# Graph attention layer: two more steps gather x alone, and VectorE and TensorE take the work of a step in another order

## What is computed

```python
hl = x @ Wl.T + bl
hr = x @ Wr.T + br
s = (jnp.take(hl, src, axis=0) + jnp.take(hr, dst, axis=0)) * alpha
s = jnp.where(s >= 0, s, SLOPE * s)
smax = jax.ops.segment_max(s, dst, num_segments=n_nodes)
e = jnp.exp(s - jnp.take(smax, dst, axis=0))
denom = jax.ops.segment_sum(e, dst, num_segments=n_nodes)
att = e / jnp.take(denom, dst, axis=0)
msg = jnp.take(x, src, axis=0) * att
# out = layernorm(x + segment_sum(msg, dst))
```

## Time and profile before

| | us |
|---|---|
| median of 3 runs | 1437.57 |
| lowest and highest run | 1435.41, 1439.32 |
| span of the profiled execution | 1129.4 |
| what lies around the span (median less span) | 308.2 |
| PE busy, weight loads busy | 1079.0, 1014.7 |
| DVE busy | 1072.6 |
| ACT busy | 998.6 |
| POOL busy | 820.7 |

### The profile page before, as it was taken

How to read it: one execution, slowest core, us unless ns; L and a number is a source line. 1 busy time by engine, 2 the same in 40 slices (tenths; PEclk the granted TensorE clock), 3 DMA queues, 4 the chain that set the end, 5 groups by cost and what they waited for, 6 DMA issues and landing times.

```text
span 1129.4 us, 34988 instructions
## 1 busy us (share of the span) xinstructions
PE 1079.0 (96%) x9403; PEld 1014.7 (90%) x9403; DVE 1072.6 (95%) x1526; ACT 998.6 (88%) x2606; POOL 820.7 (73%) x858
## 2 busy tenths in 40 slices
PE   6879999999999999999999999999999999999984
PEld 5779999999999999999999999999999899999863
DVE  7889999999999999999999999999999999999967
ACT  4359999999999999999999999999999889998996
POOL 5577777777777777777777777777777777777770
PEclk9889999999999999999999999999999999999997
DMA  9887776666667776767766666677676666676533
GB/s 227 290 221 191 192 187 191 190 188 188 191 187 191 189 189 187 192 189 190 189 189 188 189 191 190 188 189 188 191 189 185 186 188 182 187 191 183 143 99 114
DMA packets 231064, 211.97 MB, mean 188 GB/s; under 512 B 46375, under 2 KB 204286, under 8 KB 230788
## 3 DMA queue, kind: packets, MB, share of 16 engines
q0 software_dynamic: 39872, 108.39, 35.5%
q1 hardware_dynamic: 190442, 100.03, 32.4%
q10 hardware_dynamic: 565, 1.33, 0.4%
HBM read 198.95 MB, written 11.47 MB: 186 GB/s over the span
## 4 chain that ended last, share of the span: by engine, by line
PE 51%; POOL 26%; issue 11%; ACT 3%; DVE 2%; DMA 0%; ACTq 0%; POOLq 0%; DVEq 0%
POOL xg L435 25%; PE ps_w L654 19%; PE ps_sT L590 11%; PE ps_u L630 9%; PE ps_z L608 5%; PE ps_q L599 2%; PE ps_u L636 2%; PE ps_qT L618 2%; ACT attr L853 1%; DVE stats L1161 1%; ACT acc L802 0%; DMA xg<-gather_rows,srcT 0%; ACT right L811 0%; DVE acc L1086 0%; ACT ex L749 0%
## 5 line engine op out<-in xcount | busy, mean ns | idle before, releaser
L435 POOL DMA_INDIRECT xg<-gather_rows,srcT x808 | 764.9, 947 | 253.0 <-issue 235.9
L654 PE MATMUL ps_w<-onehot,ex 128*128 128x128 f32 x3328 | 405.7, 275 | 1.2 <-ACT acc L806 1.2
L654 PEld LDWEIGHTS ps_w<-onehot,ex 128*128 128x128 f32 x3328 | 388.4, 192 | 1.8 <-issue 1.6
L1095 DVE TENSOR_TENSOR_SCAN ps_F<-line,B,ps_sT 128x512 f32<-128x512 bf16 x208 | 266.1, 1279 | 1.0 <-issue 1.0
L1100 DVE TENSOR_TENSOR_SCAN B<-line,ps_F 128x512 f32<-128x512 bf16 x208 | 254.0, 1221 | 7.2
L630 PEld LDWEIGHTS ps_u<-right,onehotT 128*128 128x128 f32 x1664 | 208.5, 192 | 18.9 <-issue 0.2
L630 PE MATMUL ps_u<-right,onehotT 128*128 x1664 | 221.1, 276 | 0.0
L802 ACT ACTIVATE acc<-ps_w 128x768 f32 x208 | 168.7, 811 | 23.5
L1105 DVE TENSOR_TENSOR z<-ps_sT,B 128x512 f32<-128x512 f32 x208 | 143.9, 692 | 7.1
L1121 DVE TENSOR_TENSOR ex<-ps_z,xg 128x512 f32<-128x512 f32 x208 | 141.7, 681 | 5.7 <-ACT ps_z L773 5.7
L1129 DVE TENSOR_TENSOR v<-ps_u,attr 128x512 f32<-128x512 f32 x208 | 141.8, 682 | 0.3
(11 more groups left out here) (264 smaller groups left out, 1164.1 us busy)
## 6 DMA issues: line engine op xcount, KB each, us to landing
attr<-edge_attr_in SPq DMA_DIRECT2D x832, 64.0 KB
line<-step_lines SPq DMA_DIRECT2D x182, 128.0 KB
xg<-gather_rows,srcT POOLq DMA_INDIRECT x808
gather_rows<-acc SPq DMA_DIRECT2D x12, 512.0 KB, 6.0
line<-soon_lines SPq DMA_DIRECT2D x26, 128.0 KB
edge<-step_lines SPq DMA_DIRECT2D x182, 4.0 KB
acc<-x_in SPq DMA_DIRECT2D x6, 448.0 KB, 7.6
xg<-x_in SPq DMA_DIRECT2D x6, 448.0 KB, 5.6
```

Of the source, the lines that this page charges most:

```text
L435: pool.indirect_dma_start(out=xg[:, k % SLOTS, i, :], out_offset=None, in_=rows_dram, in_offset=bass.IndirectOffsetOnAxis(ap=srcT[:, k * W ...
L654: last = nc.tensor.matmul(columns, ex[:, (k - 1) % 2, c, i, :], onehot[:, (k - 1) % 3, i, :], start=(i == 0), stop=(i == WIDE - 1), skip_g ...
L1095: V.tensor_tensor_scan(ps_F[:, :], line[:, k % LINES, 0:GE], ps_sT[:, :], B[:, (k - 1) % 3, GE - 1:GE], ALU.add, ALU.max).then_inc(F_ok, 1)
```

## The change

- `AHEAD` is 8 instead of 6: steps 6 and 7 gather x alone too. They need two more transposes, copies and products by Wl; POOL's loop over whole rows begins with step 8. PE's `ahead` waits for the copy before the last one from k = 5 on (`ahead_sb`, k - 1). `ahead(5)`, `ahead(6)` and `ahead(7)` stand one behind another after `body(0)`, on PE and on ACT.
- The negated borders of `lines` are made by ScalarE instead of VectorE, one `body` later than ScalarE's two other parts stood; VectorE's `body(-2)` and `body(-1)` stand inside its preparation of the lines; the square lies in `ex` instead of `v`.
- VectorE's `body(k)`: F, B, h, z, v, message.
- TensorE's `body(k)`: sT, qT, u, z, q, sums.
- POOL waits for `v_ok` of step k - lead + 1 instead of `z_ps` of step k - lead.

The number of instructions on PE and ACT stays as it is but for the kinds; the diff's core:

```diff
-    AHEAD = 6
+    AHEAD = 8
...
-        sq = v[0:PR, :, :, :].rearrange("p a i d -> p a (i d)")
+        sq = flat(ex[:, 1, :, :, :])[0:PR, :].rearrange("p (a d) -> p a d", a=2)
...
+                if k == 7:
+                    pool.wait_ge(srcf_ok, 2)
+                    pool.wait_ge(step_ok, 1)
                 for i in range(WIDE):
                     pool.indirect_dma_start(
                         out=xg[:, k, i, 0:D], out_offset=None, in_=x,
...
             for k in range(AHEAD, STEPS):
-                if k == 7:
-                    pool.wait_ge(srcf_ok, 2)
-                    pool.wait_ge(rel_ok, 1)
+                if k == AHEAD:
                     pool.wait_ge(ahead_ps, 3)
-                if k == 8:
                     pool.wait_ge(u_ps, 2)
...
                 if k >= lead:
-                    pool.wait_ge(z_ps, k - lead + 1)
+                    pool.wait_ge(v_ok, k - lead + 2)
...
-                if k == 5:
-                    pe.wait_ge(ahead_sb, 4)
+                if k >= 5:
+                    pe.wait_ge(ahead_sb, k - 1)
...
-                if has(k):
-                    j = k % EDGES
...
-                    last.then_inc(q_ps, 1)
-                    pe.wait_ge(z_ok, k + 1)
...
-                    last.then_inc(z_ps, 1)
                 if has(k + 4):
                     j = (k + 4) % EDGES
...
                     last.then_inc(u_ps, 1)
+                if has(k):
+                    pe.wait_ge(z_ok, k + 1)
...
+                    last.then_inc(z_ps, 1)
+                    j = k % EDGES
...
+                    last.then_inc(q_ps, 1)
                 if k == STEPS - 1:
                     opening(0)
...
                 if k == 0:
-                    ahead(5)
+                    for a in range(5, AHEAD):
+                        ahead(a)
...
-                if k == -4:
+                if k == -3:
                     act.wait_ge(rel_ok, 1)
+                    nc.scalar.activation(lines[:, :, 0, :], halves(diff), ACT.Copy, scale=-BIG).then_inc(high_ok, 1)
+                    act.wait_ge(rel_ok, 2)
...
-            V.tensor_scalar(diff[:, :, 0], row(12), -1.0, 1.0, ALU.mult, ALU.add)
+            V.tensor_scalar(diff[:, :, 0], row(12), -1.0, 1.0, ALU.mult, ALU.add).then_inc(rel_ok, 1)
+            body(-2)
...
             V.tensor_tensor(sq, halves(rel2), halves(rel2), ALU.mult).then_inc(sq_ok, 1)
-            V.tensor_scalar(lines[:, :, 0, :], halves(diff), -BIG, None, ALU.mult).then_inc(lines_ok, 1)
+            body(-1)
```

More of the change, by code:

```diff
@@ L638, in body @@
                     last.then_inc(u_ps, 1)
+                if has(k):
+                    pe.wait_ge(z_ok, k + 1)
+                    if k == 0:
+                        pe.wait_ge(src_sb, 2)
+                    if k >= 1:
+                        pe.wait_ge(msg_ok, k)
+                    for i in range(WIDE):
+                        last = nc.tensor.transpose(ps_z[:, i * D:(i + 1) * D], z[:, k % 2, i * P:(i + 1) * P], ident[:, :])
+                    last.then_inc(z_ps, 1)
+                    j = k % EDGES
+                    if k >= 1:
+                        pe.wait_ge(oh_ok, k)
+                    for i in range(WIDE):
+                        last = nc.tensor.matmul(ps_q[:, i * P:(i + 1) * P], edge[:, j, i * P:(i + 1) * P], node[:, :],
+                                                start=(i == 0), stop=(i == WIDE - 1), skip_group_check=True)
+                    last.then_inc(q_ps, 1)
                 if k == STEPS - 1:
@@ L823, in _ @@
                     nc.scalar.activation(lines[:, :, 2, :], sq, ACT.Copy).then_inc(high_ok, 1)
-                if k == -3:
-                    act.wait_ge(lines_ok, 4)
+                if k == -2:
+                    act.wait_ge(lines_ok, 3)
+                    act.wait_ge(high_ok, 3)
                     act.dma_start(line_dram[SOON:STEPS].rearrange("(p s) c -> p (s c)", s=2),
@@ new lines, in body @@
+            def body(k):
+                if has(k):
+                    dve.wait_ge(line_in[k % LINES], 16 * (k // LINES + 1))
+                    dve.wait_ge(sT_ps, k + 1)
+                    if k >= 1:
+                        dve.wait_ge(B_ok, k)
+                    V.tensor_tensor_scan(ps_F[:, :], line[:, k % LINES, 0:GE], ps_sT[:, :],
+                                         B[:, (k - 1) % 3, GE - 1:GE], ALU.add, ALU.max).then_inc(F_ok, 1)
+                    dve.wait_ge(F_ok, k + 1)
+                    if k >= 2:
+                        dve.wait_ge(gap_ok, k - 1)
+                    V.tensor_tensor_scan(B[:, k % 3, ::-1], line[:, k % LINES, GE:0:-1], ps_F[:, ::-1], -BIG,
+                                         ALU.add, ALU.max).then_inc(B_ok, 1)
+                if has(k + 2):
+                    j = (k + 2) % SLOTS
+                    dve.wait_ge(rows_in[j], 16 * (WIDE - 1) * ((k + 2) // SLOTS + 1))
+                    dve.wait_ge(u_ps, k + 3)
+                    if k + 2 < AHEAD:
+                        V.tensor_tensor(u_of(ps_u), u_of(ps_u), both[:, :, :].broadcast_to([P, WIDE, D]), ALU.add).then_inc(h_ok, 1)
+                    else:
+                        V.tensor_tensor(u_of(ps_u)[:, 1:WIDE, :], u_of(ps_u)[:, 1:WIDE, :], xg[:, j, 1:WIDE, D:ROW], ALU.add)\
+                            .then_inc(h_ok, 1)
+                if has(k):
+                    dve.wait_ge(B_ok, k + 1)
+                    if k >= 2:
+                        dve.wait_ge(z_ps, k - 1)
+                    V.tensor_tensor(z[:, k % 2, :], ps_sT[:, :], B[:, k % 3, :], ALU.subtract).then_inc(z_ok, 1)
+                if has(k + 2):
+                    j = (k + 2) % ATTRS
+                    dve.wait_ge(attr_in[j], 64 * ((k + 2) // ATTRS + 1))
+                    dve.wait_ge(h_ok, k + 3)
+                    if k >= 0:
+                        dve.wait_ge(sT_ps, k + 1)
+                    V.tensor_tensor(v[:, k % 2, :, :], u_of(ps_u), attr[:, j, :, :], ALU.mult).then_inc(v_ok, 1)
+                if k == STEPS:
+                    ratio(0)
+                if has(k - 1):
+                    dve.wait_ge(e2_ok, k)
+                    if k >= 3:
+                        dve.wait_ge(sums_ps, k - 2)
+                    V.tensor_tensor(ex[:, (k - 1) % 2, 1, :, :], u_of(ps_z),
+                                    xg[:, (k - 1) % SLOTS, :, 0:D], ALU.mult).then_inc(msg_ok, 1)
+                if k == STEPS:
+                    for c in range(1, EARLY):
+                        ratio(c)
@@ L1067, in _ @@
             sources(0)
-            dve.wait_ge(high_ok, 2)
+            dve.wait_ge(high_ok, 3)
             V.tensor_tensor(lines[:, :, 3, :], sq, lines[:, :, 2, :], ALU.subtract).then_inc(lines_ok, 1)
@@ L1134, in _ @@
-            u_of = lambda bank: bank[:, :].rearrange("p (i d) -> p i d", i=WIDE)
-            for k in range(-2, STEPS + 1):
+            for k in range(STEPS + 1):
                 body(k)
```

81 lines of the change are left out of this document (14 added, 67 removed).

## The result

The changed kernel takes 1781.75 us (median of 4 runs, 1770.91 to 1784.11), the kernel before beside it 1438.44 us (4 runs, 1435.41 to 1439.35). The ratio is 1.239, with a 95% interval of 1.2345 to 1.2435. The forecast was 1443.6 us and a range up to 1452: wrong by far.

What follows compares the result with a forecast made beforehand. VectorE was taken to bound two thirds of the loop, GpSimd the rest. Span 1129.4 - 0.3 (start) + 5.6 (loop) + 0.7 (last part) = 1135.4; with 308.2 around it 1443.6 us, range 1434.5 to 1452.

Steps and rivals of the forecast that it cites:

- with the 308.2 that lie around the profiled span: Last step of the sum: 308.2 us outside the profiled span, added to the forecast span of 1135.4 to give 1443.6.
- `v_ok` instead of `z_ps` lets GpSimd go a step earlier and is never last while slots bind: GpSimd's gate in the loop: gathers may go a step earlier, but gather slots decide; no time was given to it.
- changes nothing in the closed loop: TensorE's new order in the loop: sT stays in front, so z, sT, F keep 2.00 us; only `ps_z` comes later.
- The loop closes through TensorE at 4.91 a step: Steps 6 to 203: F waits 0.19 us for sT each step; 4.91 us a step, +5.6 us in all.
- its four parts: VectorE's step in the loop: z to F 2.00, F to B 1.31, B to h 1.14, h to z 0.46 us.
- The waits for rows: In the loop, VectorE's h waiting for GpSimd's gathered rows: 8.7 us, forecast to go.
- A: Rival, loop: F doesn't wait for sT and GpSimd's gathers end it; about 1436 us, not slower; chance 0.15.
- B: Rival, loop: slot wait not met, GpSimd keeps most of its 7.8 us head start; 1429.8 to 1433 us; chance 0.05.
- C: Rival, VectorE's loop: h doesn't start early behind scan B; B to h 1.26, step 5.03, 1467 us; chance 0.10.
- The start, -0.3: Up to F of step 6: at 96.0 against 96.25, so -0.3 us, bounds -3 and +2.
- The last part, +0.7: Behind step 203: ScalarE is never idle and its exp comes later; +0.7 us, between 0 and 1.

## Why the prediction was wrong, point by point

**The step that failed first** is "with the 308.2 that lie around the profiled span". A span of 1129.4 and a median of 1437.57 don't belong to the same kind of execution. The prediction took the difference for a constant and added it. In the runs of the changed kernel 1.8 to 3.0 us lie around it. The two spans of the kernel before, 1129.4 and 1409.9, are 280.5 us apart: 261.5 of it between F of step 6 and F of step 203 (1.33 us in each of 197 steps, 6.21 less 4.88), 17.8 ahead of that and 1.2 behind it. This is time inside the program, in waits that the first trace hardly contains. Every term was priced in a condition in which TensorE's signals come at once. The times to be forecast came from the other.

**The term that carries the miss** follows from it, and the sum had it at nothing: "`v_ok` instead of `z_ps` lets GpSimd go a step earlier and is never last while slots bind". On a chip without late signals it is worth nothing indeed (ratio 0.9994, 0.9996 and 1.0003 on three chips). On one with them it costs 26% by itself: GpSimd waits 687.2 us for v in 133 places. The prediction put no bound on this edit, for lack of a row in which the gate was last. No rival had it. TensorE's order, of which it says that it "changes nothing in the closed loop", costs 5% there by itself, and 1.45% on a chip without late signals (a step of 4.96 in place of 4.88).

**Right, where the trace's condition held.** On the chip without late signals the changed kernel took 0.20% longer (0.09 to 0.31); the sum said 6.0 us on 1129.4, or 0.5%. From span to span, 1129.4 and 1137.0, it is 7.6 us, but the kernel before is itself slower beside the second: 1134.07 us, where a span of 1129.4 stands for some 1131.2 (1.8 around it). Some 3 us of the 7.6, and of the terms below, may be that. The terms of the sum, span to span:

- *The loop closes through TensorE at 4.91 a step*: it does, at 4.90, with each of its four parts within 0.02. The waits for rows are gone. From F of step 6 to F of step 203: 964.3 us, against 961.7 before and 967.3 forecast. So +2.6 in place of +5.6: 0.015 us of the step, 197 times.
- *Rivals A, B and C*: no drift and no step under 4.89 in mid-loop, so not A; the gathers of step 10 waited 5.18 us for their slot, to 76.78, so not B; B to h 1.13, so not C. The section of the Trainium skill that the prediction weighed, "The DRAIN you can't avoid" in "VectorE: DVE Perf Modes", says that the next instruction waits for the pipe to be empty, and also that one that is not held starts earlier. The trace shows the second, behind a scan too: h starts 0.09 us before the backward scan ends.
- *The start, -0.3*: +3.9. F of step 6 stood at 100.19, before at 96.25. F of step 0 did come earlier (63.79 against 66.67), though not at 62.2. Then sT of step 2 started at 77.40, forecast 73.5. TensorE had been idle 3.33 us ahead of sT of step 1, and its granted clock was at 1.2 GHz from 66.68 to 73.51. Two windows of 5 us, with the columns of the earlier trace rows:

```profile
65.00:70.00 5.00, 2.34 (x10) 2.22 (x11) 3.38 (x6) 0.78 (x2) 3.78 (x5) 0.67 0.79 250
70.00:75.00 5.00, 5.00 (x33) 4.84 (x31) 3.65 (x5) 1.62 (x4) 1.30 (x2) 0.65 0.86 197
```

  Each product of u took 1.92 us there and not 1.05. From the start of sT of step 1 (67.66) to z of step 0 (73.23) it was 5.57 us; by the spacings of the same work at 2.4 GHz (0.44 and 0.43 for sT, 0.22 for qT, 0.89 for each product) it would be some 2.9. So about 2.7 of the 3.9 us by which sT of step 2 is behind the forecast are the clock's; the rest was there when sT of step 1 started (67.66, forecast 66.4). In the kernel before, the clock was at that level from 58.04 to 64.86 and full from there on. The working moved instructions to another time but kept the durations of the place they came from.
- *The last part, +0.7*: from F of step 203 to the end of the span 72.5 us, before 71.4, so +1.1.

That the four parts of the closed loop came out within 0.02 us shows the mechanism of the loop to be right. That the span's +7.6 us lies near the sum's +6.0 is in part luck: the start was forecast 4.2 us too low and the loop 3.0 too high.

## What to carry to other kernels

Check the span of the profiled execution against the median before anything else: here 1.8 to 3.0 us lie around a span, and a difference of 308 meant a profile of another kind of execution, on which no sum could forecast the median. As far as these runs go, a gate between engines is safer on a signal that is held back with the rest (z, let go with the others) than on one that another engine makes out of them (v): v is early when all is well and gains nothing, and comes several instructions later when the signals are late. Of the parts run on chips without late signals the only one that paid was the head start of eight, with the lines by ScalarE (0.9985, 0.9974 to 0.9995); it wasn't run alone on a chip with late signals, nor VectorE's order alone on one without.

## What the runs showed of the hardware

- The kernel before took 1129.8 to 1135.7 us on three chips and 1409 to 1439 us on others, with TensorE's signals 0.014 us behind its matmuls on the former. On the latter they came 0.6 to 2.1 us late in the median, by signal, in the kernel before, and up to 19 us. No recorded signal of VectorE or ScalarE was late.
- Traces of the latter hold 10,043 to 17,838 records of semaphore updates, those of the former 35,675 to 36,040, with all the instructions in both.
- The late signals stand only where GpSimd issues indirect gathers without a break, or less than 2 us behind such a row, and mostly for matmuls that end more than 2 us after its start. In a row of sixteen TensorE's own issue slowed down with them, from 2.00 us for the sixteen matmuls of the sums to 17.8.
- On a chip with late signals the changed kernel, with idle gaps of 5 us on TensorE, had a mean granted clock of 0.866 of full speed; where they came in time it was 0.986.
